# The first source tile of attention heads two to seven, bounded and multiplied by the edge counts on GpSimd

## The reference

```
h = (x @ W.T).reshape(n, heads, out_ch)
e = leaky_relu(a_src[src] + a_dst[dst], 0.2)
ex = exp(e - segment_max(e, dst)[dst])
alpha = ex / (segment_sum(ex, dst)[dst] + EPS)
out = segment_sum(alpha[:, :, None] * h[src], dst)
```

## Time and profile before

| what | value |
|---|---|
| median of 3 executions | 1713.73 us (1713.4 to 1713.74) |
| the profiled execution: its own time | 1713.25 us |
| the profiled execution: its span | 1711.5 us |
| mean granted TensorE clock | 0.994 |
| busy share of PE, DVE, ACT, POOL | 98%, 54%, 26%, 41% |
| chain that ended last, by engine | PE 85%, DVE 11%, ACT 2%, issue 1% |

### The profile page before, as it was taken

The page is one execution under the profiler, slowest core; times in us unless marked ns, Lnnn a source line. Parts: engine busy times, 40 slices in busy tenths (PEclk is TensorE's granted clock), DMA queues, the critical chain, the costliest instruction groups (busy, mean ns, idle before and its releaser), DMA issues.

```text
span 1711.5 us, 25768 instructions
## 1 busy us (share of the span) xinstructions
PE 1670.7 (98%) x10227; PEld 1572.0 (92%) x10227; DVE 920.4 (54%) x1860; ACT 451.3 (26%) x867; POOL 698.9 (41%) x432
## 2 busy tenths in 40 slices
PE   8799999999999999899999999999999999999999
PEld 7699999997999999899477889899999999999999
DVE  8993636517776689777488444513112141226731
ACT  7443213303223147834132311101001111112310
POOL 1026955661544631340020365441643435342663
PEclk9899999999999999999999999999999999999999
DMA  2002222323212210015010121110211111111222
GB/s 91 1 29 65 76 65 66 136 88 139 65 47 65 75 47 19 20 29 151 11 33 1 33 81 60 54 48 28 84 57 54 56 47 56 56 49 38 66 74 73
DMA packets 42000, 99.84 MB, mean 58 GB/s; under 512 B 10508, under 2 KB 12142, under 8 KB 41894
## 3 DMA queue, kind: packets, MB, share of 16 engines
q1 hardware_dynamic: 37828, 87.87, 16.6%
q10 hardware_dynamic: 4066, 10.46, 1.7%
HBM read 96.39 MB, written 1.92 MB: 57 GB/s over the span
## 4 chain that ended last, share of the span: by engine, by line
PE 85%; DVE 11%; ACT 2%; issue 1%; POOL 0%; DVEq 0%; POOLq 0%; ACTq 0%
PE bank L2543 10%; PE bank L2545 10%; PE bank L2544 10%; PE banks L2543 9%; PE banks L2545 9%; PE banks L2544 9%; PE bank L3039 3%; PE banks L3039 3%; PE bank L3214 3%; PE bank L3219 3%; PE banks L3214 2%; PE banks L3219 2%; PE bank L2963 2%; DVE src_hot L1599 1%; DVE tmp L1935 1%; PE banks L2644 1%
## 5 line engine op out<-in xcount | busy, mean ns | idle before, releaser
L904 POOL TENSOR_TENSOR w_hi<-raw,ones_r 128x768 fp32r<-128x768 f32 (+1 forms) x192 | 298.0, 1552 | 905.4 <-PE banks L2545 311.3
L907 POOL TENSOR_TENSOR w_lo<-raw,w_hi 128x768 fp32r<-128x768 f32 (+1 forms) x192 | 369.6, 1925 | 15.1
L2543 PE MATMUL bank<-w_hi,xT_hi 128*125 128x384 f32 (+2 forms) x573 | 191.8, 335 | 1.9 <-DVE small L2076 1.5
L2545 PE MATMUL bank<-w_hi,xT_lo 128*125 128x384 f32 (+2 forms) x573 | 190.7, 333 | 0.0
L2544 PE MATMUL bank<-w_lo,xT_hi 128*125 128x384 f32 (+2 forms) x573 | 190.5, 333 | 0.0
L2543 PE MATMUL banks<-w_hi,xT_hi 128*125 128x384 f32 (+2 forms) x427 | 147.9, 346 | 0.0
L2545 PE MATMUL banks<-w_hi,xT_lo 128*125 128x384 f32 (+2 forms) x427 | 147.5, 345 | 0.0
L2544 PE MATMUL banks<-w_lo,xT_hi 128*125 128x384 f32 (+2 forms) x427 | 147.5, 345 | 0.0
L2543 PEld LDWEIGHTS bank<-w_hi,xT_hi 128*125 128x125 f32 x573 | 106.4, 186 | 5.1 <-DVE small L2076 1.7
L2438 DVE TENSOR_TENSOR through_lo<-bank,through_hi 125x384 fp32r<-125x384 f32 (+1 forms) x45 | 25.6, 578 | 155.3 <-ACT through_hi L1459 155.3
L2544 PEld LDWEIGHTS bank<-w_lo,xT_hi 128*125 128x125 f32 x573 | 106.4, 186 | 2.4
(11 more groups left out here) (620 smaller groups left out, 3933.1 us busy)
## 6 DMA issues: line engine op xcount, KB each, us to landing
raw<-wa SPq DMA_DIRECT2D x92, 384.0 KB, 3.0
raw<-wc SPq DMA_DIRECT2D x76, 384.0 KB, 3.0
raw<-wb SPq DMA_DIRECT2D x28, 448.0 KB, 3.3
w_rows<-w_in ACTq DMA_DIRECT2D x1, 3072.0 KB, 12.8
bias<-bias_in ACTq DMA_DIRECT2D x6, 384.0 KB
w_first<-w_in ACTq DMA_DIRECT2D x1, 2304.0 KB, 11.2
w_down<-w_down_in SPq DMA_DIRECT2D x8, 288.0 KB, 5.4
w_up<-w_up_in SPq DMA_DIRECT2D x1, 2304.0 KB, 10.9
```

What stands on the lines that cost most here:

```text
L904: pool.tensor_tensor(w_hi[:, k, 0:width], raw[:, k, 0:width], ones[:, 0:1].to_broadcast([P, width]), ALU.mult).then_inc(S("unit_high"), 1)
L907: pool.tensor_tensor(w_lo[:, k, 0:width], raw[:, k, 0:width], f(w_hi[:, k, 0:width]), ALU.subtract).then_inc(S("unit_split"), 1)
L2543: tell_used(pe.matmul(dst, l_hi, r_hi, start=start, stop=False))
L2545: return pe.matmul(dst, l_lo, r_hi, start=False, stop=stop)
```

## The change

For heads 2 to 7, tile 0 is taken out of VectorE's first product. GpSimd does that tile in two operations: it bounds the tile at 3.0 in place (`tensor_scalar` with min), waits for that operation's own semaphore, and multiplies the tile by `adj[:, 0]` in place (`tensor_tensor`). It may start when the first exponential of the head is done. TensorE's product waits for one more semaphore, `g2p_first_tile`, before it reads tile 0. The four `hT_lo` subtractions stay on GpSimd, each ahead of the pair of heads 4 to 7. All that follows is unchanged; the number of VectorE's instructions too.

```diff
--- before.py
+++ after.py
@@ -934,11 +934,18 @@
             second = FIRST_UNIT["d", "g2b"]
             for u in range(after, second):
                 split(UNIT, n_shared)(u, u // RING, u % RING)
-            for h in range(POOL_LOWS):
-                pool.wait_ge(*E("g2p_high", h + 1))
-                pool.wait_ge(*E("g2p_prob", len(PARTS) * (h + 4)))
-                pool.tensor_tensor(hT_lo[:, h, 0:NODES], head_T[:], f(hT_hi[:, h, 0:NODES]), ALU.subtract
-                                   ).then_inc(S("g2p_low"), 1)
+            for h in range(2, HEADS):
+                if h >= HEADS - POOL_LOWS:
+                    done = h - HEADS + POOL_LOWS
+                    pool.wait_ge(*E("g2p_high", done + 1))
+                    pool.wait_ge(*E("g2p_prob", len(PARTS) * h))
+                    pool.tensor_tensor(hT_lo[:, done, 0:NODES], head_T[:], f(hT_hi[:, done, 0:NODES]), ALU.subtract
+                                       ).then_inc(S("g2p_low"), 1)
+                pool.wait_ge(*E("g2p_powers", NT * h + 1))
+                first = prob_of("g2p", h)[:, 0]
+                pool.tensor_scalar(first, first, 3.0, None, ALU.min).then_inc(S("g2p_first_bound"), 1)
+                pool.wait_ge(*E("g2p_first_bound", h - 1))
+                pool.tensor_tensor(first, first, f(adj[:, 0]), ALU.mult).then_inc(S("g2p_first_tile"), 1)
             pool.wait_ge(*E("g2p_prob", len(PARTS) * HEADS))
@@ -2128,7 +2135,7 @@
-                for a, b in PARTS:
+                for a, b in ((1, PARTS[0][1]), PARTS[1]):
                     dve.wait_ge(*E("g2p_powers", NT * h + b))
                     STT(pr[:, a:b], pr[:, a:b], 3.0, f(adj[:, a:b]), ALU.min, ALU.mult).then_inc(S("g2p_prob"), 1)
 
@@ -2957,6 +2964,8 @@
                         at = (n - a) * (HEAD_DIM + 1)
                         for s in range(NT):
                             if n == 0 and s == PARTS[0][0]:
+                                if h >= 2:
+                                    pe.wait_ge(*E("g2p_first_tile", h - 1))
                                 pe.wait_ge(*E("g2p_prob", len(PARTS) * h + 1))
```

## The result

The changed kernel takes 1716.54 us in the median of 21 executions (1714.9 to 1717.34), the kernel before 1713.13 in 21 beside them (1711.34 to 1714.42). The ratio is 1.0018, with a 95% interval of 1.0013 to 1.0024: 3.1 us slower (2.2 to 4.1); the two medians lie 3.4 apart. I had forecast 1713.3 with a range of 1712.0 to 1715.6, a gain of 0.45 us. The profiled execution has a span of 1714.7 against 1711.5, with the same mean clock of 0.994.

A forecast was written before the change was run, and what follows sets the result against it. TensorE, busy 98%, waits in heads 2 to 7 on a path through VectorE. Three passes of 0.20 us give 0.60, of which 0.45 arrives: from the median 1713.73 to 1713.3, range 1712.0 to 1715.6.

The forecast's parts named there:

- The stage: Heads 2 to 7, 47.4 us, where TensorE waits and VectorE is busy 46.3; a saving was to count there.
- S to T: Start of a head's maxima to end of the following reciprocal on VectorE: 7.73 us before, forecast 7.53 after.
- T to S: From that reciprocal's end over mean, product, spreading and copy to the maxima two heads later than the one finished: 7.79 us.
- The ceiling: VectorE's second product must wait for the last exponential, making S to T 7.34; of 0.67 us at most 0.39 stays.
- the cheapest pair: GpSimd's bound and product at lowest prices, 2.17 us with hand-overs: S to T 7.39, gain 0.7 to 1.0, time 1712.7.
- the price of GpSimd's bound at 3.0: GpSimd's first operation on tile 0, taken at 0.70 us, between IOTA's 0.66 and a two-input operation's 1.29.
- The pair with its hand-overs: GpSimd's bound and product on tile 0 plus hand-overs, 2.32 us expected, ending at S + 4.33 (S: start of maxima).
- the rival at 0.25: GpSimd's pair, beyond 2.52 us, delays VectorE's first product more than was saved: 1713.8 to 1717.8, middle 1715; chance 0.25.
- The mechanism: In heads 3, 5 and 7, VectorE's first product, due at S + 3.90, is held by GpSimd's product until S + 4.33.
- The dearest case: GpSimd's pair at 3.22 us: S to T 8.44, VectorE alone sets the pace, 4.1 us late in all, 1717.8.
- The delay at GpSimd's first one-input operation: GpSimd's first `tensor_scalar`, in head 2, starts late once; beyond 4.1 us slack it delays head 2's product; chance 0.05.
- After that TensorE is full, so nothing takes the 0.45 back: Behind head 7's product, starting 0.45 us earlier, everything was to move alike and the whole gain to stay.

The follow-up runs named there:

- Experiments 2 to 4: Changed kernel with GpSimd's bound alone (1711.65 us) or product alone (1710.13), product moved behind VectorE's second product (1713.16), neither operation (1710.91).
- Experiment 6: GpSimd's product behind VectorE's second product for heads 2 to 6 only, head 7 on VectorE as in the kernel before: 1712.21 us, ratio 0.9992.
- experiment 3: Changed kernel with GpSimd's product put behind VectorE's second product, TensorE taking tile 0 last in its first node tile: 1713.16 us, ratio 0.9998.
- the late version: The kernel of experiment 3, all six heads: changed kernel with GpSimd's product behind VectorE's second product; 1713.16 us, ratio 0.9998.
- the product-only run: Changed kernel without GpSimd's bound at 3.0, tile 0 only multiplied by the counts: 1710.13 us, ratio 0.9979.
- bound only: Changed kernel without GpSimd's product, tile 0 bounded at 3.0 but not multiplied by the counts: 1711.65 us, ratio 0.9991.
- neither: Changed kernel with tile 0 of heads 2 to 7 neither bounded nor multiplied on any engine: 1710.91 us, ratio 0.9986.
- experiment 2: Two runs of the changed kernel: GpSimd's bound without its product, 1711.65 us (ratio 0.9991); its product without the bound, 1710.13 us (0.9979).

## Why the prediction was wrong

**The frame held.** The stage, the three engines on the path, S to T of 7.73 and T to S of 7.79 were read rightly, and 3.03 us of the loss of 3.1 to 3.4 lie in that stage. The maxima are not slowed by GpSimd (3.96 to 3.98 in every run). The ceiling was right as well: without a collision S to T is 7.34, as worked out, limited by the last exponential. The stage then gains 0.96 to 0.99, at the upper end of the 0.7 to 1.0 given for the cheapest pair.

**The step that failed is the price of GpSimd's bound at 3.0**, "I take 0.70, near the IOTA", and with it the upper bound "a two-input operation, 1.29, is the upper one". It measured 1.78 alone: an operation with two inputs is no upper bound for one with one input. The product was taken at 1.40 and is 1.53. The pair with its hand-overs, 2.32 in the forecast and 3.22 as the dearest, is 0.10 + 1.77 + 0.09 + 1.53 = 3.49 before any waiting. That lies past the 2.52 that I had named as the point from which it is slower, so the rival at 0.25 is what happened. The pair is dearer than its dearest, while the time, 1716.54, lies within its 1713.8 to 1717.8.

**The mechanism was right in kind and wrong in place.** I expected VectorE's first product to be held by GpSimd's product. With the longer bound the order turned: VectorE's first product got in ahead, held GpSimd's product by 0.39, and that one then held the second product by 0.86. The sum for head 5 is 5.06 until the second product is ready, 0.86 of holding, 2.04 and 0.44: 8.40. Of the 1.06 above 7.34 the holding is 0.86. The other 0.20 follows from it: the exponentials stand behind the mean of the head before, and that mean now waits for VectorE's late reciprocal (694.55, 0.10 after S, instead of 0.08 before it). The dearest case had put head 3's maxima 0.7 late and its T 1.4, and four heads at 8.44 behind that: 4.1 in all. Measured were 0.05 and 0.71, as head 2 was held by only 0.45, and then four heads at 8.34 instead of 7.76: 0.71 + 4 x 0.58 = 3.03. Experiments 2 to 4 show that the loss is this meeting and nothing else. What the two engines share in it no run shows: the "port" in the expectation of experiment 3 was an assumption, and measured is the waiting alone (2.98 instead of 2.12, 1.92 instead of 1.53). Experiment 6 shows what the idea gives where the meeting is avoided: 0.5 us by the trace.

**The delay at GpSimd's first one-input operation did not come.** Head 2's bound started at 672.16, 0.08 after the first exponential ended (671.25 + 0.83), and took 1.78 like the others.

**"After that TensorE is full, so nothing takes the 0.45 back"** was too simple. In the changed kernel the shift was passed on whole. But the late version lost 0.76 of its 0.96 in the dense stage behind. And the time moves with whether TensorE's clock falls later on, which in the product-only run goes with some 2.7 us, more than the change could bring.

What stays open: what brings the lower clock between 820 and 860 us. Three kernels with a stage of about 47.2 gained 2.2 (bound only), 3.7 (product only) and 2.3 us (neither) over the kernel before, and a fourth, the late one, 0.7. The runs show that the time goes with the clock, not what sets the clock off.

## What to carry to other kernels

Before moving an operation to an idle engine, price that very operation there. An operation of another kind, even one that seems to do more, is no upper bound (here 1.78 us with one tensor input against 1.53 with two); if the trace has none, a few of them at the end of the program cost one run. Then draw where each of its operations will stand against the instructions on the other engine with two SBUF inputs, and look in a trace which of them hold each other: here the product did (2.98 us instead of 2.12) and the bound did not (0.80). A pair that misses its slot need not cost its own overrun; it can come to stand in front of the longer instruction behind. And a saving of less than a microsecond should be followed to the next stage's start in the trace, since the total time moved by more than that with the granted clock here (up to 3.9 us between 0.993 and 0.995).

## What the runs showed of the hardware

- GpSimd, f32, 626 columns on 125 partitions: one tensor input with a constant 1.78 to 1.80 us (min or multiplication), 313 columns 1.00; two tensor inputs 1.53; a column spread over the tile as second input 1.23; writing a constant 0.62.
- GpSimd's product and VectorE's products with both inputs in SBUF held each other until the end of the instruction under way, either way round (VectorE's second product 2.98 instead of 2.12, GpSimd's product 1.92 instead of 1.53). The waiting time stands inside the instruction's own duration, and the later one, reckoned from its price alone, started 0.11 to 0.16 us before the profile's end of the earlier. The maxima, with one input in PSUM, took 3.98 with and without GpSimd beside them. The bound reads one SBUF tensor, and VectorE's product issued in its midst took 0.80, with the bound at 1.78 (experiment 2).
- Executions of one kernel (27 of the kernel before) differed by up to 3.9 us with the mean granted clock between 0.993 and 0.995. Between 820 and 860 us the clock fell in some profiled executions (mean 0.91, as low as 0.50 in a slice of 2 us) and not in others (1.00), with TensorE busy 38.6 to 38.7 of 40 us in both.
